# Layer norms of a four-layer Flamingo block: root and reciprocal over 128x512 in place of a power over 128x4 and a spread

## The reference

```python
def _layernorm(x, axis=-1, eps=1e-05):
    m = jnp.mean(x, axis=axis, keepdims=True)
    v = jnp.var(x, axis=axis, keepdims=True)
    return (x - m) / jnp.sqrt(v + eps)
...
x = x + tanh(g_xattn[0]) * scan_gate(_layernorm(x), ctx, ctx)      # q * (decayed running sum of k*v)
x = x + tanh(g_ffn[0])   * moe_gelu_top2(_layernorm(x))            # 8 experts, hidden 512
x = x + tanh(g_xattn[1]) * attention_16_heads(_layernorm(x), ctx)
x = x + tanh(g_ffn[1])   * moe_silu_gated_top2(_layernorm(x))      # 8 experts, hidden 352
x = x + tanh(g_xattn[2]) * pair_attention(_layernorm(x), ctx)
x = x + tanh(g_ffn[2])   * moe_silu_gated_top4(_layernorm(x))      # 16 experts, hidden 128
x = x + tanh(g_xattn[3]) * attention_16_heads(_layernorm(x), ctx)
x = x + tanh(g_ffn[3])   * moe_gelu_shared_top2(_layernorm(x))     # 8 + 1 experts, hidden 512
```

## Time and profile before

| | us |
|---|---|
| median of 3 runs (587.42 to 590.1) | 588.36 |
| the profiled execution | 593.04 |
| its span, first to last instruction | 591.3 |
| TensorE busy | 561.5 (95%) |
| VectorE busy | 441.2 (75%) |
| ScalarE busy | 402.5 (68%) |
| GpSimd busy | 102.0 (17%) |

### The profile page before, as it was taken

The page is one execution under the profiler, slowest core; times in us unless marked ns, Lnnn a source line. Parts: engine busy times, 40 slices in busy tenths (PEclk is TensorE's granted clock), DMA queues, the critical chain, the costliest instruction groups (busy, mean ns, idle before and its releaser), DMA issues.

```text
span 591.3 us, 8732 instructions
## 1 busy us (share of the span) xinstructions
PE 561.5 (95%) x3258; PEld 388.0 (66%) x3258; DVE 441.2 (75%) x692; ACT 402.5 (68%) x561; POOL 102.0 (17%) x69
## 2 busy tenths in 40 slices
PE   8999999898999999999896999999999999999997
PEld 5688887656777867764330346566546767888886
DVE  3477988768749799986889676676768938787786
ACT  3799899765856755426999774624514858888875
POOL 5400000001110000004989703200000310000000
PEclk8999999999999999999899899999999999999999
DMA  6118020300100459110000024505610110812100
GB/s 241 39 36 321 37 71 1 116 1 2 55 1 2 162 209 262 48 52 1 7 1 1 1 72 103 184 3 163 158 35 2 38 38 2 314 46 70 35 2 35
DMA packets 19342, 43.81 MB, mean 74 GB/s; under 512 B 2090, under 2 KB 7594, under 8 KB 19300
## 3 DMA queue, kind: packets, MB, share of 16 engines
q1 hardware_dynamic: 19300, 43.25, 23.1%
HBM read 42.55 MB, written 0.70 MB: 73 GB/s over the span
## 4 chain that ended last, share of the span: by engine, by line
PE 72%; DVE 15%; ACT 8%; issue 3%; POOL 1%; DVEq 0%; ACTq 0%; POOLq 0%
PE ps L818 35%; ACT work L1217 5%; PE ps L860 4%; PE ps L800 3%; PE ps L569 3%; PE ps L552 3%; DVE h_lo L1754 2%; PE ps L844 2%; PE ps L846 2%; PE ps L885 2%; PE ps L845 2%; PE ps L685 2%; PE ps L559 2%; PE ps L658 2%; DVE h_act L1727 2%
## 5 line engine op out<-in xcount | busy, mean ns | idle before, releaser
L1754 DVE TENSOR_TENSOR h_lo<-h_act,h_hi 128x512 fp32r<-128x512 f32 (+1 forms) x114 | 103.7, 914 | 39.8 <-ACT h_hi L1264 39.0
L818 PE MATMUL ps<-n_hi,w_hi 128*128 128x512 f32 x224 | 86.6, 421 | 2.4 <-DVE h_act L1727 1.2
L1264 ACT CAST h_hi<-h_act 128x1024 fp32r<-128x1024 f32 (+1 forms) x88 | 75.4, 856 | 14.6 <-PE ps L818 11.9
L818 PE MATMUL ps<-n_hi,w_lo 128*128 128x512 f32 x224 | 79.7, 391 | 0.0
L818 PE MATMUL ps<-n_lo,w_hi 128*128 128x512 f32 x224 | 79.5, 390 | 0.0
L1967 POOL TENSOR_TENSOR rstd<-var_eps,minus_half 128x4 f32<-128x4 f32 x16 | 17.1, 1070 | 312.8 <-DVE var_eps L1409 312.8
L1217 ACT ACTIVATE work<-work,p_rest 128x2048 f32<-128x2048 f32 x31 | 59.4, 1994 | 0.4 <-DVE work L1607 0.4
L1257 ACT ACTIVATE h_act<-ps 128x512 f32<-128x512 f32 x44 | 26.3, 598 | 45.6 <-PE ps L818 45.3
L818 PE MATMUL ps<-h_hi,w_hi 128*128 128x512 f32 x162 | 56.3, 396 | 0.1
L1994 POOL TENSOR_TENSOR work<-xc,txt 128x2048 f32<-128x2048 f32 x15 | 54.0, 3624 | 9.2 <-ACT xc L1181 7.9
L818 PE MATMUL ps<-h_hi,w_lo 128*128 128x512 f32 x162 | 55.4, 390 | 0.0
(11 more groups left out here) (235 smaller groups left out, 1043.2 us busy)
## 6 DMA issues: line engine op xcount, KB each, us to landing
work<-g_rows SPq DMA_DIRECT2D x36, 512.0 KB, 5.8
w_f<-in_w SPq DMA_DIRECT2D x20, 512.0 KB, 3.6
w_f<-in_w SPq DMA_DIRECT2D x8, 384.0 KB, 3.3
work<-g_rows SPq DMA_DIRECT2D x8, 256.0 KB, 7.0
work<-g_rows SPq DMA_DIRECT2D x4, 384.0 KB, 6.7
diag<-in_w SPq DMA_DIRECT2D x2, 512.0 KB, 5.1
work<-in_w SPq DMA_DIRECT2D x2, 512.0 KB, 4.5
w_f<-in_w_rest SPq DMA_DIRECT2D x2, 384.0 KB, 4.1
```

Source lines behind the costliest of these rows:

```text
L818: mm = pe.matmul(dst[i], wap(wt, e, lo, size, rows), mv[i], start=(first and c == 0), stop=(last and c == 2))
L1264: act.copy(places(h_hi, m, step), places(h_act, m, step)).then_inc(s["hi"], 1)
L1754: dve.tensor_tensor(lo, src, hi.bitcast(F32), ALU.subtract).then_inc(s["lo"], 1)
```

## The change

It concerns norms 0, 1, 3 and 7 (`ROOTED`), both halves of each; norms 2, 4, 5 and 6 keep the power. In the rooted norms the variance is one product of a 128x128 matrix of ones with `sq` (128x512), which leaves the sum over the features on every partition. ScalarE takes the root of sum/128 + epsilon in place in PSUM (`norm_root`, the Sqrt table), VectorE the reciprocal in place over 128x512, and then multiplies. norm_eps, norm_power and norm_spread do nothing for these norms. VectorE's norm_out(3, 0) and norm_out(7, 0) take norm_eps's place ahead of update(1). ScalarE's order around norm 1 changes (two weight casts go behind the second root), its table loads for Silu and Gelu after the attentions move behind the second root, and loads of Sqrt and Gelu are added. Two more keep_busy products stand behind project(1).

```diff
+ROOTED = (0, 1, 3, 7,)
...
+        eps_w = sb("eps_w", [P, 1])
...
+        LNBANK.update({(j, 1): (1, 5, 5) for j in ROOTED if j})
...
-        table = sb("table", [P, 1])
+        table = sb("table", [P, 9])
...
-        ln = {k: sem(f"ln_{k}") for k in ("mean", "xc", "sq", "var", "eps", "rstd", "bc", "n", "hi", "lo")}
+        ln = {k: sem(f"ln_{k}") for k in ("mean", "xc", "sq", "var", "std", "eps", "rstd", "bc", "n", "hi", "lo")}
...
         def query_part(p):
...
+        def nth_power(j, t):
+            return 2 * (j - len([o for o in ROOTED if o < j])) + t + 1
+        def nth_root(j, t):
+            return 2 * ROOTED.index(j) + t + 1
         def halves_of(t):
...
             def norm_var(j, t):
...
+                if j in ROOTED:
+                    pe.matmul(ps[:, LNBANK[j, t][1]], ones_w[:, :], sq[:, half(t)], start=True, stop=True).then_inc(ln["var"], 1)
+                    return
...
             def norm_spread(j, t):
-                pe.wait_ge(ln["rstd"], 2 * j + t + 1)
+                if j in ROOTED:
+                    return
+                pe.wait_ge(ln["rstd"], nth_power(j, t))
...
                 turn_out(PAIRS - 1)
                 keep_busy(2, 1)
                 project(1)
-                keep_busy(2, 1)
+                keep_busy(4, 1)
             def weights_out(t, r):
...
             norm_var(1, 1)
...
-            norm_spread(1, 1)
...
             def norm_copy(j, t):
...
+            def norm_root(j, t):
+                act.wait_ge(ln["var"], 2 * j + t + 1)
+                var = ps[:, LNBANK[j, t][1]]
+                act.activation(var, var, ACT.Sqrt, bias=eps_w[:, 0:1], scale=1.0 / P).then_inc(ln["std"], 1)
             def norm_high(j, t):
                 act.wait_ge(ln["n"], 2 * j + t + 1)
...
                 if j == 3:
                     act.wait_ge(pre["txt"], 1)
...
+                norm_root(j, 1)
+                act.activation(table[:, 7 + j // 7:8 + j // 7], ones_w[:, 0:1], ACT.Silu if j == 3 else ACT.Gelu)
             def load_table(function):
-                act.activation(table[:, :], minus_half[:, 0:1], function)
+                at_col = (ACT.Exp, ACT.Gelu, ACT.Silu, ACT.Sqrt).index(function)
+                act.activation(table[:, at_col:at_col + 1], ones_w[:, 0:1], function)
             def copy_values(i, q):
...
                     if p == PAIRS - 1:
                         norm_square((3, 7)[i], 0)
+                act.activation(table[:, 5 + i:6 + i], ones_w[:, 0:1], ACT.Sqrt)
+                norm_root((3, 7)[i], 0)
                 out_copy(PAIRS - 2)
                 norm_copy((3, 7)[i], 0)
                 out_copy(PAIRS - 1)
-                load_table((ACT.Silu, ACT.Gelu)[i])
             def softmax_exp(t):
                 act.wait_ge(x2["soft"], t + 1)
...
             act.wait_ge(in_pack["p_first"], 16)
...
+            load_table(ACT.Sqrt)
             for t in range(2):
                 norm_square(0, t)
             act.wait_ge(in_ctx, 16)
             for t in range(2):
...
+                norm_root(0, t)
                 norm_copy(0, t)
             split_hi_up(MOES[0], 0)
             copy_values(0, 0)
...
             norm_square(1, 0)
             norm_copy(1, 0)
             copy_keys(0, 0, 0)
-            split_hi_down(MOES[0], 0)
+            norm_root(1, 0)
             copy_keys(0, 0, 1)
             norm_square(1, 1)
             norm_copy(1, 1)
-            split_hi_up(MOES[0], 1)
             norm_high(1, 0)
             copy_keys(0, 1, 0)
+            norm_root(1, 1)
+            act.activation(table[:, 4:5], ones_w[:, 0:1], ACT.Gelu)
+            split_hi_down(MOES[0], 0)
+            split_hi_up(MOES[0], 1)
             copy_keys(0, 1, 1)
             split_hi_down(MOES[0], 1)
...
             def norm_eps(j, t):
+                if j in ROOTED:
+                    return
...
             def norm_out(j, t):
-                dve.wait_ge(ln["bc"], 2 * j + t + 1)
                 dve.wait_ge(ln["xc"], 2 * j + t + 1)
+                if j in ROOTED:
+                    dve.wait_ge(ln["std"], nth_root(j, t))
+                    root = ps[:, LNBANK[j, t][1]]
+                    link(dve.reciprocal(root, root))
+                    dve.tensor_tensor(n[:, half(t)], xc[:, half(t)], root, ALU.mult).then_inc(ln["n"], 1)
+                    return
+                dve.wait_ge(ln["bc"], nth_power(j, t))
...
             def norm_low(j, t):
...
                     if p == PAIRS - 2:
                         update(0)
-                norm_eps((3, 7)[i], 0)
+                norm_out((3, 7)[i], 0)
                 update(1)
...
-                norm_out(j, 0)
+                if L == 0:
+                    norm_out(j, 0)
                 norm_low(j, 0)
-                norm_eps(j, 1)
                 if m.gated:
...
                     norm_out(j, 1)
...
+            dve.memset(eps_w[:, :], EPS)
...
             def norm_power(j, t):
+                if j in ROOTED:
+                    return
...
-                pool.wait_ge(ln["eps"], 2 * j + t + 1)
+                pool.wait_ge(ln["eps"], nth_power(j, t))
...
             def low_weights(m, e, part):
```

## The result

The changed kernel takes 614.75 us (median of 6 executions, 610.36 to 618.58), the kernel before beside it 589.73 (6, 587.42 to 591.57). The ratio is 1.041, 95% interval 1.0374 to 1.0446. On the 588.36 of the forecast that is 612.5 us; forecast were 607.3 in a range of 599 to 614. It is slower, as expected, but by some 24 us instead of 18.9: inside the range, near its upper end.

A forecast was written before the change was run, and what follows sets the result against it. TensorE was taken to set the pace for most of the span, with chains of short waiting steps at the changed norms' entries. 15.5 us there plus 3.4 for the clock gave +18.9 on 588.4: 607.3 us, range 599 to 614.

The forecast's parts named there:

- the chain: Lateness at the start and the ends of attentions 0 and 1: 4.3 + 6.9 + 4.3 = 15.5 us.
- the reciprocal: On VectorE over 128x512: 3.37 us by a straight line through two narrower widths, 3.4 with its wait.
- the start: Norms 0 and 1: later x and n make TensorE's up(4) wait for n_lo until 35.6 instead of 31.34, +4.3 us.
- attention 0: End of attention 0, norm 3: table load, product(0) and reciprocal all in one line, the dearest place, +6.9 us.
- attention 1: End of attention 1, norm 7: same steps, but the table load runs beside the reciprocal, +4.3 us.
- rival (b): Late engines catch up in stages behind with unseen slack, half of the 15.5 regained: 596 us, chance 0.08.
- what costs nothing: The eps_w memset and longer keep_busy lie in TensorE's idle time; nothing else waited for GpSimd's eight powers; no DMA touched.
- (a): The wide reciprocal on VectorE runs like an ordinary operation, 0.69 us: 586 us, faster; chance 0.03.
- (c): The reciprocal on VectorE costs eight column times, 4.4 us: 8 us more, 615 us; chance 0.05.
- (d): ScalarE's table loads cost twice their row where ScalarE is full before them: 5 us more, 612 us; chance 0.05.
- the clock term: TensorE's longer idleness lowers its clock: two half-speed stretches on the path, 3.4 us, bounds 0 and 8.5.
- low case (e): TensorE's clock stays up though the sum is right: 604 us, inside the forecast's own chance of 0.76.

The follow-up runs named there:

- the warming: Changed kernel with unread bf16 products on a constant tile in TensorE's five gaps before waits for VectorE: ratio 1.0316 to the kernel before, 608.41 us.
- the kernel with the start alone: Changed kernel with root and reciprocal in norms 0 and 1 only, the other norms as before: ratio 1.0113 to the kernel before, 596.91 us.
- the narrow kernel: Changed kernel with root and reciprocal over 128x4 at all four norms, before the spread, which stays: ratio 1.001 to the kernel before, 591.17 us.

## Why the prediction was right or wrong

**Right: what bounds it, and the chain.** 15.5 us forecast, 14.7 measured by matched instructions and 14.3 by the intercepts (up to 17.3 if half clock costs only what the warming gave back). By its steps: the reciprocal 3.364 (3.37); x of half 1 at the start done at 22.28 (22.9), up(4) at 35.14 (35.6); x of half 1 in attention 0 late by 2.9 on top of the lateness it came with (3.1), the silu by 3.4 (4.1), the second logits by 6.5 (6.9), TensorE's gap there 4.74 (4.9); in attention 1 x late by 3.0 (3.2), the gelu by 4.1 (4.1), VectorE's place at up(4) by 4.4 (4.3). The start came out 0.5 cheaper because the scan began at 8.52, not 9.13: the first norm_mean products took 1.88 us in this execution and 2.48 in before's. That up(4) comes so near is in part luck. The forecast had ScalarE's n_hi as the late one (34.8); it was there at 33.48, and the h_lo of 1.50 us on VectorE, which the forecast does not have, held n_lo instead. The full row of TensorE held, too:

```profile
45.00:60.00 15.00, 15.00 (x71) 12.38 (x70) 9.45 (x10) 13.52 (x15) 0.00 (x0) 1.00 0.67 228
```

After has the same full 15 us, and the lateness stays what it was. That refutes rival (b), as does the kernel with the start alone: its intercept is 3.7 us above before's at the end of the whole span.

**Right: what costs nothing.** GpSimd's busy time falls from 102.0 to 93.3; its share of the chain was 1% before and is 0% after. The moved Sqrt load at 168.45 in attention 0 was hidden.

**The other rivals.** (a) and (c) fall with 3.364 us: by width it is 177 ns for 4 columns, 250 for 16, 552 for 64, 1764 for 256 and 3364 for 512, one line of 6.3 ns a column, six column times of 1.04. The Trainium skill (VectorE: DVE Perf Modes, First, the fixed hardware budget) has a repeat count of 8 for the reciprocal; read as eight column times, an estimated 4.4 us, it isn't borne out. (d) falls with 1.283 us a load: at 180.71 the load starts and the silu behind it begins at 182.12, 1.41 later with the trigger between. The load starts 0.02 us behind the root. The half of 2.66 us that the Trainium skill counts as a drain (ScalarE: Activation LUTs, What ACT_TABLE_LOAD costs) is not seen.

**Wrong: the clock term.** Forecast 3.4 with bounds of 0 and 8.5; measured 10.2 us on average by the slope, above the upper bound, and 7.1 by what the warming gave back: two to three times the forecast either way. The mechanism was named (TensorE's new waits lower its clock), its size was not. Three steps of the reasoning failed. First, it counted falls from one trace of 591.3 us, as if a kernel had its falls; h differs from one execution to the next (20.7 to 41.9 us over the six of after), and the profiled pair happened to differ by 2.7. Second, it took one stretch of 3.4 us for a gap; the one behind the 4.74 us lasted 6.8. Third, it took only gaps of 2 us and more as causes; falls came behind 1.32 and 0.89 too, and whether one comes there isn't decided by the gap alone. The bounds came from the count of the gaps that I foresaw, when the unknown was how often a stretch behind each is halved.

The range held with some luck: at a mean clock like that of before the change would have cost 14.7 and the time would have been 603, near the forecast's low case (e); the other 7 to 10 us came from the term that was put at 3.4, and the upper end of 614 was wide enough for them only because all falls together and the table loads of (d) had been let in.

**Still open.** What decides that the clock falls in one execution and not in another at the same place with the same waits. How the 24 us divide between chain and clock, within the two figures given. Whether the slow h_lo of the start would be gone with GpSimd's work placed elsewhere.

## What to carry to other kernels

A reciprocal costs by the column, six times an ordinary VectorE operation (6.3 against 1.04 ns), so do root and reciprocal on the narrow form and spread the result (here that was as fast as the power, not faster); saving a TensorE product that others hide doesn't pay for 3.36 us on a chain. When an edit makes TensorE wait, price it twice: the wait, and the half clock that follows. Take the mean clock of several executions, not the falls in one trace, and fit span against half-clock time to part the two; the line prices falls that lie in or ahead of waits too high. When a function table load is moved from cover to behind a step, look at what stands queued behind it: alone it cost 0.2 us at most in the narrow kernel, but with product(0) behind it and the long reciprocal behind that, the order cost 1 to 2 us at attention 0. And when work is moved on one engine, see what runs beside it on the others then.

## What the runs showed of the hardware that was not expected

- A microsecond at half clock goes with 0.42 us of the span, over 70 executions of before (slope 0.43) and six of after (0.41). In a stretch that TensorE filled (187.5 to 192.7 in after) it cost 0.5: 5.3 us took 2.6 more. In the fall at 15.4, ahead of a wait for VectorE, it cost nothing.
- Executions of one kernel differ in their half-clock time by a factor of two (20.7 to 41.9 us after), and that is most of the scatter in their times.
- Stretches at half clock last 3.4 or 6.8 us in the traces here. One began behind a wait of 0.89 us that in another kernel had no fall behind it.
- Products that nobody reads cut the half-clock time from 30.9 to 10.7 us and the mean span by 5.9 us, without holding up the chain in the trace.
- The first norm_mean products of a kernel took 1.88 us in one execution, 2.48 and 2.65 in others, at a granted clock of 1.00 in all three, and what follows is shifted by about as much. A difference of half a microsecond between two traces is no effect of an edit unless the starts agree.
- A VectorE h_lo of 128x512 took 1.50 us beside GpSimd's w_lo, and 0.69 with GpSimd idle.
